# Four-layer graph network on one core: the one-time constants of the recurrent half, and where six pieces of work stand in three engines' orders

## The reference, cut to what matters

```
x = layernorm(x + L0(x, adj))     # row scalings and one dense layer
x = layernorm(x + L1(x, adj))     # graph product, two dense layers with batch norm
x = layernorm(x + L2(x, adj))     # two graph convolutions, then four LSTM passes
x = layernorm(x + L3(x, adj))     # h = x @ fc.T + b, then 8 Euler steps:
#   h = h + dt*(alph*0.5*(adj@h - h) + h @ w_eff - h + x),  w_eff = (w * clip(d)) @ w.T
```

## Time and profile before

| | us |
|---|---|
| median of 3 runs | 937.22 |
| lowest, highest | 935.61, 937.93 |
| profiled execution: its time | 935.11 |
| profiled execution: its span (first to last instruction) | 933.3 |

### The profile page before, as it was taken

How to read it: one execution, slowest core, us unless ns; L and a number is a source line. 1 busy time by engine, 2 the same in 40 slices (tenths; PEclk the granted TensorE clock), 3 DMA queues, 4 the chain that set the end, 5 groups by cost and what they waited for, 6 DMA issues and landing times.

```text
span 933.3 us, 14540 instructions
## 1 busy us (share of the span) xinstructions
PE 893.1 (96%) x4990; PEld 774.3 (83%) x4990; DVE 671.3 (72%) x1589; ACT 564.8 (61%) x1230; POOL 327.6 (35%) x531
## 2 busy tenths in 40 slices
PE   9899999988989899999999999999999999999996
PEld 6788886366777689989989898998889898978986
DVE  6789996776687676677676767767776777675744
ACT  6477675944655565477457647765774775476341
POOL 3856554820122511362144216303521531340121
PEclk9999999999999899999999999999999999999999
DMA  5321201320110101001101200120110001001000
GB/s 186 136 68 62 74 36 46 135 87 6 34 58 1 34 1 57 2 23 35 57 1 46 69 1 12 35 69 1 46 39 31 12 12 46 1 12 34 1 23 24
DMA packets 26595, 38.55 MB, mean 41 GB/s; under 512 B 3333, under 2 KB 12422, under 8 KB 26010
## 3 DMA queue, kind: packets, MB, share of 16 engines
q1 hardware_dynamic: 26088, 36.05, 11.5%
q10 hardware_dynamic: 434, 1.57, 0.5%
HBM read 21.89 MB, written 15.73 MB: 40 GB/s over the span
## 4 chain that ended last, share of the span: by engine, by line
PE 50%; DVE 10%; ACT 8%; POOL 7%; issue 3%; ACTq 0%; DVEq 0%; POOLq 0%
PE psum L141 14%; PE psum L143 14%; PE psum L142 14%; PE psum L1867 2%; PE psum L1863 2%; PE psum L1864 2%; ACT gate L1438 2%; POOL out_rstd L1371 1%; ACT raw L1469 1%; POOL node_l L1389 1%; POOL x_rstd L1371 1%; ACT x L1469 1%; ACT raw L1532 1%; DVE cell L1584 1%; ACT gate L1441 1%
## 5 line engine op out<-in xcount | busy, mean ns | idle before, releaser
L1438 ACT ACTIVATE gate<-psum,gate_bias 128x256 f32<-128x256 f32 (+2 forms) x296 | 143.8, 557 | 67.7 <-PE psum L1867 54.4
L141 PE MATMUL psum<-in_h,wih_h 128*128 128x256 f32 (+2 forms) x312 | 106.8, 342 | 8.7 <-DVE in_l L1605 5.0
L143 PE MATMUL psum<-in_h,wih_l 128*128 128x256 f32 (+2 forms) x312 | 103.5, 332 | 0.0
L142 PE MATMUL psum<-in_l,wih_h 128*128 128x256 f32 (+2 forms) x312 | 103.1, 330 | 0.0
L141 PEld LDWEIGHTS psum<-in_h,wih_h 128*128 128x128 f32 x312 | 59.0, 189 | 21.2 <-DVE in_l L1605 8.6
L1405 POOL TENSOR_TENSOR gate<-in_h,in_l 128x512 f32<-128x512 f32 x14 | 17.9, 1306 | 157.5 <-DVE in_l L1605 157.5
L1441 ACT ACTIVATE gate<-cell 128x512 f32<-128x512 f32 (+2 forms) x80 | 40.3, 503 | 49.5 <-DVE cell L1589 39.1
L1586 DVE TENSOR_TENSOR gate<-gate 128x256 f32<-128x256 f32 (+2 forms) x48 | 24.1, 502 | 58.8 <-ACT gate L1438 58.7
L141 PE MATMUL psum<-e_h,shared 128*128 128x384 f32 x180 | 62.0, 344 | 2.2 <-POOL e_l L1420 2.0
L142 PEld LDWEIGHTS psum<-in_l,wih_h 128*128 128x128 f32 x312 | 59.2, 190 | 5.1 <-issue 0.2
L143 PEld LDWEIGHTS psum<-in_h,wih_l 128*128 128x128 f32 x312 | 58.9, 189 | 4.7
(11 more groups left out here) (394 smaller groups left out, 2894.2 us busy)
## 6 DMA issues: line engine op xcount, KB each, us to landing
x_spill<-x SPq DMA_DIRECT2D x30, 256.0 KB, 2.0
xt<-in_x_t_dram SPq DMA_DIRECT2D x16, 256.0 KB, 2.6
raw<-x_spill SPq DMA_DIRECT2D x16, 256.0 KB, 2.8
o_spill<-xt SPq DMA_DIRECT2D x14, 256.0 KB, 2.0
xt<-o_spill SPq DMA_DIRECT2D x14, 256.0 KB, 3.4
x<-x_spill SPq DMA_DIRECT2D x14, 256.0 KB, 3.6
out_dram<-raw SPq DMA_DIRECT2D x14, 256.0 KB, 2.3
raw<-in_adj_t_dram ACTq DMA_DIRECT2D x1, 1024.0 KB, 8.8
```

What stands on the lines that cost most here:

```text
L141: pe.matmul(dst, lh, rh, start=start, stop=False, **kw)
L142: pe.matmul(dst, lh, rl, start=False, stop=False, **kw)
L143: return pe.matmul(dst, ll, rh, start=False, stop=stop, **kw)
L1438: nc.scalar.activation(gate[q][:, 0:n], banks[GATE_BANK[q]][:, 0:n], ACT.Tanh if q == 2 else ACT.Sigmoid, bias=gate_bias[:, p - 1, q:q + 1 ...
```

## The change

Three things are edited. In step 0, PE's and DVE's slot 5 holds `turn_1` ahead of `fc_1`, and ACT's `norm_1` goes from slot 6 (between cells 6 and 7) to slot 7 (between cells 7 and 8). In step 1, the copy of `vec_t` goes from DVE to ACT, first in slot 1. Also in step 1, `mix_4` and `mix_5` stand in DVE's slot 1 (around `bias`), `mix_6` and `mix_7` first in slot 2, and `split_e` goes from slot 3 to slot 2 on ACT (behind `norm_0`) and on POOL (between `norm_0` and `x3sum_1`).

```
-  ONCE_PE:   ["fc_1", "turn_1"]                       +  ["turn_1", "fc_1"]          (slot 5)
-  ONCE_DVE:  ["fc_1", "turn_1"]                       +  ["turn_1", "fc_1"]          (slot 5)
-  ONCE_ACT:  ["gather1_0", "second_2", "norm_1"], []  +  ["gather1_0", "second_2"], ["norm_1"]   (slots 6, 7)
-  NEXT_ACT = FILL_ACT[:3] + [["power1_0", "power2_0", "evens_l", "gather0_0", "split_e"],
+  NEXT_ACT = [[], ["lift"] + FILL_ACT[1], FILL_ACT[2] + ["split_e"], ["power1_0", "power2_0", "evens_l", "gather0_0"],
-  NEXT_DVE = [[], ["lift", "turn_0", "bias", "mix_4"], ["x3t_0", "mix_5", "x3sum_1", "mix_6", "mix_7"],
+  NEXT_DVE = [[], ["turn_0", "mix_4", "bias", "mix_5"], ["mix_6", "mix_7", "x3t_0", "x3sum_1"],
-  NEXT_POOL = FILL_POOL[:3] + [["split_e"]] + FILL_POOL[4:]
+  NEXT_POOL = FILL_POOL[:2] + [["norm_0", "split_e", "x3sum_1"]] + FILL_POOL[3:]
+            def lift():                                   # on ACT; DVE's lift() goes
+                act.wait_ge(vt_done, 1)
+                nc.scalar.copy(vec_t, UB[0][0:ROWS, :]).then_inc(vt_kept, 1)
```

More of the change, by code:

```diff
@@ L1237, in second_half @@
         ONCE_PE = [[], ["turn_0", "first_3", "square"], ["cube", "second_0"], ["gather0_0", "fourth", "second_1"],
-                   ["weight0_0", "fc_0"], ["fc_1", "turn_1"], ["gather1_0", "fc_2", "second_2"], ["weight1_0"],
+                   ["weight0_0", "fc_0"], ["turn_1", "fc_1"], ["gather1_0", "fc_2", "second_2"], ["weight1_0"],
                    ["gather0_1"], ["weight0_1", "second_3"], ["gather1_1", "offset", "weight1_1"]]
         ONCE_ACT = [["prep_0"], ["first_3"], ["norm_0", "evens_h", "second_0"], ["evens_l", "gather0_0", "second_1"],
-                    ["rest_h", "prep_1", "weight0_0"], ["rest_l"], ["gather1_0", "second_2", "norm_1"], [],
+                    ["rest_h", "prep_1", "weight0_0"], ["rest_l"], ["gather1_0", "second_2"], ["norm_1"],
                     ["input_0", "gather0_1"], ["weight0_1", "second_3"], ["gather1_1", "ahead_0", "input_1"]]
         ONCE_DVE = [[], ["turn_0", "first_3", "square"], ["cube", "second_0"], ["gather0_0", "fourth", "second_1"],
-                    ["weight0_0", "fc_0"], ["fc_1", "turn_1"], ["gather1_0", "fc_2", "second_2", "mix_0"],
+                    ["weight0_0", "fc_0"], ["turn_1", "fc_1"], ["gather1_0", "fc_2", "second_2", "mix_0"],
                     ["weight1_0", "mix_1"], ["gather0_1", "input_0", "mix_2"], ["weight0_1", "second_3", "mix_3"],
@@ L1251, in second_half @@
                    ["weight0_0", "coefs0_0"], ["coefs1_0", "turn_1"]] + FILL_PE[6:]
-        NEXT_ACT = FILL_ACT[:3] + [["power1_0", "power2_0", "evens_l", "gather0_0", "split_e"],
-                                   ["rest_h", "prep_1", "weight0_0", "coefs0_0", "x3norm_1"],
-                                   ["coefs1_0", "x3split_1", "rest_l"]] + FILL_ACT[6:]
-        NEXT_DVE = [[], ["lift", "turn_0", "bias", "mix_4"], ["x3t_0", "mix_5", "x3sum_1", "mix_6", "mix_7"],
+        NEXT_ACT = [[], ["lift"] + FILL_ACT[1], FILL_ACT[2] + ["split_e"], ["power1_0", "power2_0", "evens_l", "gather0_0"],
+                    ["rest_h", "prep_1", "weight0_0", "coefs0_0", "x3norm_1"],
+                    ["coefs1_0", "x3split_1", "rest_l"]] + FILL_ACT[6:]
+        NEXT_DVE = [[], ["turn_0", "mix_4", "bias", "mix_5"], ["mix_6", "mix_7", "x3t_0", "x3sum_1"],
                     ["power1_0", "power2_0", "gather0_0"], ["weight0_0", "coefs0_0"], ["coefs1_0", "turn_1"]] + FILL_DVE[6:]
-        NEXT_POOL = FILL_POOL[:3] + [["split_e"]] + FILL_POOL[4:]
+        NEXT_POOL = FILL_POOL[:2] + [["norm_0", "split_e", "x3sum_1"]] + FILL_POOL[3:]
         def step(g, cell_step, pieces, fill, lstm=True, l3=True, front=True, done=True):
@@ L1567, in _ @@
                             "rest_h": lambda g: rest(g, False), "rest_l": lambda g: rest(g, True),
-                            "x3t": x3t, "out": out_piece, "outhalf": out_half, "split_e": split_e,
+                            "x3t": x3t, "out": out_piece, "outhalf": out_half, "split_e": split_e, "lift": lift,
                             "first": lambda t: high(0, t), "second": lambda t: high(1, t),
@@ L1818, in offset @@
                 nc.vector.tensor_copy(bc, UB[1][0:ROWS, 0:2 * D]).then_inc(bc_kept, 1)
-            def lift():
-                dve.wait_ge(vt_done, 1)
-                nc.vector.tensor_copy(vec_t, UB[0][0:ROWS, :]).then_inc(vt_kept, 1)
             def bias():
@@ L1834, in _ @@
                             "columns": columns, "conv_bias": conv_bias_rows, "row_sum": row_sum, "weff": weff, "bcols": spread_bias, "square": square, "cube": cube,
-                            "fourth": fourth, "fc": fc, "mix": mix, "offset": offset, "lift": lift, "bias": bias, "first": lambda t: low(0, t), "second": lambda t: low(1, t),
+                            "fourth": fourth, "fc": fc, "mix": mix, "offset": offset, "bias": bias, "first": lambda t: low(0, t), "second": lambda t: low(1, t),
                             "input": layer_input}, START_DVE, ONCE_DVE, NEXT_DVE, FILL_DVE, LAST_DVE, TAIL_DVE)
```

## The result

| | before | after |
|---|---|---|
| median of 6 runs each, us | 937.14 | 929.37 |
| lowest, highest | 935.06, 937.93 | 928.12, 931.59 |
| profiled execution: time | 935.11 | 931.06 |
| profiled execution: span | 933.3 | 928.5 |

The ratio is 0.9930, with a 95% interval of 0.9918 to 0.9942: 5.4 to 7.7 us less. The forecast was 931.4 with a range of 928.2 to 934.9, so the change came out faster, as forecast, and 2.0 under the forecast time. (The two medians alone differ by 7.8, a quotient of 0.9917, just outside that interval; six runs of each spread over 3 us.

What follows compares the result with a forecast made beforehand. PE, busy for 96% of the span, was taken as the bound, so only its waits and slow-clock stretches count. Median: 937.22 + 0.3 (step 0) - 3.1 (lift) - 3.0 (mixes and split) = 931.4, range 928.2 to 934.9.

Steps and rivals of the forecast that it cites:

- Lift: Step 1, wait ahead of `bias`: copy of `vec_t` on ACT lets `x3t_0` start sooner, gain 3.4 (bounds 1.7 to 4.4).
- both of my bounds: Cost of the `vec_t` copy on ACT in step 1: bounds 0.57 and 0.67 us, taken as 0.63.
- Mixes and split: Step 1, `e` ready sooner: the 1.99 wait at `coefs0_0` goes and its slow clock's 1.7, gain 3.6 to 3.7.
- The two margins: Step 1: ACT 1.0 in hand before cell 3's gates; POOL's split on cell 3's DVE work, state up to 0.4 later.
- Step 0: Step 0, waits ahead of `fc_1` and cell 8 replaced by 1.3 and about 1.5: loss 0.15, taken as 0.3.
- the swap: Step 0: `turn_1` moved into the 0.78 wait ahead of `fc_1`, gain 0.35.
- The sum: Whole kernel: 928.2 for the profiled execution, 931.4 for the median, counting clock falls only in part.
- 1 (the clock eats it): Clock falls ahead of `bias` and in step 0, each 1.7, leave 935.2; chance 0.17.
- 2 (no hold-up for `mix_4`): Step 1: POOL doesn't hold up `mix_4` and no clock fall, 927.2 or about 928.5 for a median; chance 0.09.
- 3: Step 1: `split_e` blocks ACT ahead of cell 3's gates, slower, 939 if the mixes slip to 328; chance 0.04.
- 4: Step 1: freed time returns as another wait, ACT or POOL late, half the gain, 934.3; chance 0.08.
- The clock rule: PE's waits: skill warns only of gaps over about 3 us; by it the 1.99 gap costs no clock, sum 932.4.

Runs made afterwards that it cites:

- e4: The changed kernel run once more, beside the kernel before on another chip's set of runs: 930.90 against 936.49, ratio 0.9934.
- e1: The kernel before with only the copy of `vec_t` moved to ACT; mixes, split and step 0 unchanged: 932.40 against 936.49, ratio 0.9949.
- e5: The changed kernel with DVE's bias copy ahead of `mix_4` in slot 1 of step 1: 931.34, ratio 0.9931 to the kernel before.
- e2: The kernel before with only the mixes and the split of `e` moved as in the change: 934.26, ratio 0.9968.
- e8: The changed kernel with `mix_0` to `mix_2` one slot later in step 0, `mix_3` in step 1, bias copy ahead of the mixes: 930.51, ratio 0.9932.
- e6: The changed kernel with ACT's `norm_1` back in slot 6, `turn_1` still ahead of `fc_1`: 931.73, ratio 0.9942 to the kernel before.
- e3: The kernel before with the step 0 edits alone: 936.75, ratio 1.0001.
- e10: The changed kernel with the low part of `e` on DVE instead of POOL and DVE's bias copy ahead of `mix_4`: 931.00 against 936.07, ratio 0.9946.
- e7: The changed kernel with `mix_0` behind cell 7 on DVE instead of in front of it: 930.23, ratio 0.9930 to the kernel before.
- e11: e8's order of the mixes, low part of `e` on DVE, `split_e` on ACT in slot 3 ahead of `gather0_0`: 928.16 against 936.07, ratio 0.9920.

## Why the prediction was right, step by step

- **Lift.** Forecast: copy ends 306.0, `bias` takes 1.85, bias copy held up by `mix_4` behind POOL, `x3t_0` 3.4 sooner. Measured from the start of the half: `bias` 2.1 sooner (111.98 to 109.92, as forecast), 1.92 long, `x3t_0` 3.2 sooner, 3.4 with step 0's 0.2 taken off. The step that decides, that DVE's copy and not PE's clock sets `x3t_0`, was right: the same 34.37 behind `gather0_1` with and without a fall (after, e4), and 0.6 (e1) to 0.95 (e5) sooner with the copy first. The copy cost ACT 0.56, below both of my bounds.
- **Mixes and split.** Forecast 3.6 to 3.7; e2 gives 3.7, the change 3.7. `coefs0_0` takes 3.19 instead of 4.77. The two margins that I named were the right ones to name: ACT has 1.2 in hand ahead of cell 3's gates (forecast 1.0), and POOL's `e_l` now lies on cell 3's first product (0.83 instead of 0.69). e5 shows the second used up, e8 both.
- **Step 0.** Forecast a loss of 0.15, with new waits of 1.3 and 1.5; measured 0.19, 1.18 and 1.49. I had the swap at +0.35 (0.41) and `norm_1` at -0.5 (-0.6).
- **The sum.** In the marks 6.87 against my 6.85 for one execution. (The prediction's line gives 928.2 for what is 928.26, and its chance of "faster" adds up to 0.82, not 0.83; neither matters.) The step that was mis-sized is the last: for the median I took 1.05 off that sum, leaving 5.8, for falls of the clock that don't come each time. The ratios ask for 6.6 and 6.2, between the two. That the forecast of one execution came out to 0.02 is partly luck: had no fall stood behind the 1.99 in the trace of before, as none did in e1's, the marks would have given 1.3 less (an estimate from the 30.7 and 29.4 of the table). In the first six runs the difference of the medians was 7.8, which is more than the marks give; the second set had 5.6. The parts of a run that the change doesn't edit move it by as much: the first half by 0.5 between these two traces and by up to 2.9 over all, a fall near 225 by 1.2 to 1.35, one near 828 by 1.5.
- **Rivals.** 1 (the clock eats it) came in part: one fall of about 3 us stands behind `bias` in after, but PE would have waited for DVE's copy in any case, so it cost nothing at `x3t_0`. Of the eleven traces with the copy on ACT, seven have a fall there. In e6 it went on past `x3t_0` and cost 1.8. 2 (no hold-up for `mix_4`) fell: the row of 1.76. 3 was seen in e8 only. 4 fell: the forecast 3.7 is there at `turn_1` of step 1, and from it on the steps are equal to 0.1.
- **The clock rule.** Behind gaps of 1.99 (before, e3) the clock fell, behind one of 1.99 (e1) it didn't, and behind the 2.1 near 828, which all fourteen traces have, it fell in four (after, e1, e4, e10) and not in the others. The Trainium skill (TensorE: Matmul & The Clock Gate, Why this matters for your kernels) warns of idle gaps on PE above about 3 us; here falls stood behind shorter ones too, and that the gap of 1.99 cost a fall is what the row of before showed, though e1 shows that it needn't.

## What to carry to other kernels

When a wait goes, ask which engine is late next and at what time, and count that engine's queue in order, with everything else that runs at the time beside it; here that gave the new start of `x3t_0` to 0.1 us, with step 0's delay taken off. A copy behind which another engine waits belongs on the engine that is free at that moment (e1: 4.8 us under). That it should also stand ahead of constant work with no deadline is shown for the start of `x3t_0` alone (e5: 0.95 sooner), not for the time. A long POOL operation with operands in SBUF should lie where DVE has no products of two SBUF operands: at one such overlap PE lost 0.4 in e5, and DVE's product was 1.4 longer in e8 (e7's loss lay elsewhere), and at `turn_1` e11, which removed it together with ACT's wait, is the only version more than 1 us ahead.

## What the runs showed of the hardware

- DVE instructions with two SBUF operands stood behind a POOL operation of 1.3 to 2.7 us: four mixes took 1.76 instead of 0.85 (after), a product 2.11 instead of 0.69 (e8). Statistics (one operand, 0.86 to 0.87) and copies from PSUM (the bias copy 1.21 in e5, 1.23 in after) ran on at their usual time beside them. A small POOL operation held up none: a product that began beside one on 128x4 (312.53 to 313.63, after) took its usual 0.69.
- The product of a six-row operand took 3.7 us at 1.2 GHz and 1.9 at 2.4. In the kernel before the clock was at 1.2 all through it and rose only in cell 2, at 314.7.
- ACT copies 6x512 from PSUM in 0.56 us and 128x512 in 0.57, where DVE takes 0.67 and 0.68.
- The granted clock is one of the largest sources of spread: the same wait in the same kernel was followed by a fall in one execution and not in the next, at 1.2 to 1.5 us each (near 225: e4, not after; near 828: after, not before).
